# Opening of the attention stage: stack loads on two DMA queues, and half of the second group's row maxima inside the first group

## The chip, the cores and the metric

One Trainium2 core runs the whole program as one launch. The metric is device time in microseconds of the one core; lower is better. The kernel before was run three times for its time and once more under the profiler.

## The reference

Two transformer-like layers on `x[4, 512, 256]` (4 batches, 512 positions, width 256, 16 heads of 16). Layer 0 is softmax attention with a linear-attention memory term mixed in by a gate, plus a mixture of 8 experts (top 2). Layer 1 is decayed linear attention in chunks of 128, plus another mixture of 8 experts (top 2):

```
xn = layernorm(x)
q, k, v = rope(xn Wq), rope(xn Wk), xn Wv                   # layer 0
mem     = elu1(q) (elu1(k)^T v) / (elu1(q) sum elu1(k))
attn    = softmax(q k^T * 16**-0.5) v                       # per batch and head, 512 x 512 scores
x = x + (g * mem + (1 - g) * attn) Wo + moe0(xn)
xn = layernorm(x)
x = x + lightning_attention(xn) Wo1 + moe1(xn)              # layer 1
```

The change touches only the softmax attention of layer 0. Its softmax is computed as exp(score - row maximum), and the row maxima are computed first, by a pass of its own over the same scores.

## The kernel before

The program has three stages with a barrier of all engines between them: `layer0_front` (layer norm, projections, rotary, the first experts), `middle` (the softmax attention of layer 0, and for each batch what follows it up to the projections of layer 1), and `layer1_main`. The second stage, `middle`, is the one that changes, and of it only the opening.

**Work of the stage.** A batch has `GROUPS = 4` groups of `HG = 4` heads, and a group has `TILES = 4` tiles of 128 positions. Queries and keys are kept as stacks of three bfloat16 parts: `qst[g]` and `kst[g]`, 96 partitions (six pieces of 16) by 4 heads by 512 positions. One stack is loaded by six DMAs of 64 KB; the values `vst[g]` by one DMA of 256 KB. All 13 raise the same semaphore `stack_in[g]`, and `LOADED = 16 * 13` is what a reader waits for.

For each group n there are two passes on TensorE:

- `rows(n, g, t, b, heads)` (line 1491): for tile t, one matmul of 96 x 512 for each head into one of the two banks of `psM`; VectorE's `reduce(n, i, t)` (line 1305) takes the maximum of each row. A bank is free again when its maximum is taken. After four tiles (16 maxima) `split_max` (lines 1313 and 1315) makes two bfloat16 parts of them, TensorE's `turn_max` (line 1498) transposes these into `psN`, VectorE copies them to `nmT` (line 1466 or 1328), and SyncE's `send_max` stores `nmT` to memory (line 1087), waits, and loads it back as two further rows of `qst[g]` (line 1089, semaphore `max_in[g]`).
- `attend(b, g, ...)` on TensorE waits for `max_in[g]`. For each tile k it forms `scores` (line 1509, heads 0 and 1, then 2 and 3), ScalarE takes the exponential (line 1242), and `values(k - 1)` (line 1518) multiplies the tile before by the values.

The loop looks ahead by two groups: while group G is attended, the rows and maxima of group G + 2 are made, two heads behind each pair of scores. So the first two groups' maxima (groups 0 and 1) have to be made in front of the loop:

```
            for t in range(TILES):
                rows(0, 0, t, 0, range(HG))
            pe.wait_ge(identb_done, 1)
            for t in range(TILES):
                rows(1, 1, t, 0, range(HG))
                if t == 0:
                    turn_max(0, 0)
```

**Order on SyncE** (all loads are issued there): group 0's stacks and values, the identity matrix, group 1's stacks and values, seven small constants (`consts_in`, the last is `gates`), `iota8`, seven weights (`weights_in`), three tables (`dispatch.load`), group 2's stacks and values, `send_max` for group 0, group 3's stacks and values, and then the loop.

**Beside it.** ScalarE waits for the constants, forms `gates` (line 1285), the decay tables (lines 1287 to 1291) and, after `weights_in`, three rounded copies of the weights (line 1295). GpSimd sets parts of `kst` to one, issues eight indirect gathers (`fetch(0)`, line 1189), forms the low parts of the weights (line 1224, semaphore `w_lo`, three in all) and then masks the decay table (line 1227). VectorE, behind the maxima of both groups, takes 1 minus the gates (line 1469) and waits for `tables` and for all three of `w_lo` before it enters the loop.

Of the kernel before, what the change touches and what calls it, by code (L numbers as in the profile page):

```python
# [24 lines left out]
TILES = SEQ // P  # L25
D = 256
KT = D // P
HEADS = 16
HD = D // HEADS
HG = 4  # L30
GROUPS = HEADS // HG
# [18 lines left out]
Q_PARTS = (0, 0, 1, 0, 2, 1)  # L50
# [78 lines left out]
class Routing:  # L129
# [17 lines left out]
    def load(self, sp, io):  # L147
        sp.dma_start(self.iota8[:, :, :], io["iota8"].rearrange("p (t e) -> p t e", e=E)).then_inc(self.iota_in, 16)
# [795 lines left out]
def middle(nc, io, scratch, keep):  # L944
# [8 lines left out]
    with ExitStack() as ctx:  # L953
# [110 lines left out]
        def second(n):  # L1064
            return psM if alone(n) else psX

        block = ctx.enter_context(nc.Block())

        @block.sync
        def _(sp):  # L1070
            def load(b, g):
                for op, dst, order in ((0, qst, Q_PARTS), (1, kst, K_PARTS)):
                    for i, part in enumerate(order):
                        row = (g % 2) * HG * HD
                        src = scratch["parts"][b, part, KT * op + g // 2, row:row + HG * HD, :]
                        sp.dma_start(dst[g][i * HD:(i + 1) * HD, :, :],
                                     src.rearrange("(h d) t -> d h t", d=HD)).then_inc(stack_in[g], 16)
                sp.dma_start(vst[g][:, :, :], scratch["v"][b, :, g * HG * VW:(g + 1) * HG * VW]
                             .rearrange("(t p) n -> p t n", p=P)).then_inc(stack_in[g], 16)

            def send_max(n, g, i, before=None):

                sp.wait_ge(nmT_copied, n)
                if before is not None:
                    sp.wait_ge(max_in[(g - 1) % GROUPS], before)

                sp.dma_start(scratch["max"], nmT[i][:, :]).then_inc(max_out, 16)
                sp.wait_ge(max_out, 16 * n)
                sp.dma_start(qst[g][STACK:STACKM, :, :],
                             scratch["max"].rearrange("(a h) t -> a h t", a=2)).then_inc(max_in[g], 16)  # L1090

            load(0, 0)
            sp.dma_start(ident[:, :], io["ident"]).then_inc(ident_in, 16)
            load(0, 1)
            for dst, src in ((after[:, :], io["after"]), (rel[:, :], io["rel"]), (causal[:, :], io["causal"]),
                             (before[:, :], io["before"]), (ldrows[:, :], io["log_decay_rows"]),
                             (ldall[:, :], io["log_decay"].to_broadcast((P, HEADS))),
# [3 lines left out]
            for dst, src in ((rqk[:, :, 0:D], "Wq1"), (rqk[:, :, D:2 * D], "Wk1"), (rv, "Wv1"),  # L1101
                             (rr[:, :, 0:E], "router1"), (rr[:, :, E:RW], "Wg1"),
                             (wo[:, :, :], "Wo0")):
                sp.dma_start(dst, io[src].rearrange("(k p) n -> p k n", p=P)).then_inc(weights_in, 16)
            sp.dma_start(wg2[:, :], io["Wg2"]).then_inc(weights_in, 16)
            dispatch.load(sp, io)
            load(0, 2)
            send_max(1, 0, 0)
            load(0, 3)

            def attend(b, g, last, beside):
# [120 lines left out]
        def _(act):  # L1232
# [46 lines left out]
            def silu_v(n):  # L1279
                act.wait_ge(v_ps, n + 1)  # L1280
                nc.scalar.activation(v32[:, :, :, 0:HD], second(n)[:, :, :].rearrange("p a (t h d) -> p (a t) h d", t=2, d=HD),
                                     ACT.Silu).then_inc(v_done, 1)

            act.wait_ge(consts_in, CONSTS)
            nc.scalar.activation(gates[:, 1, :], gates[:, 1, :], ACT.Sigmoid).then_inc(g_done, 1)
            for k in range(KT):
# [13 lines left out]
        def _(dve):  # L1300
# [17 lines left out]
            def attend(b, g, last, beside):  # L1318
                G = GROUPS * b + g
                ahead = not (last and g >= GROUPS - 2)  # L1320
                for t in range(TILES):
                    if ahead:
                        reduce(G + 2, g % 2, t)
                    if t == 0 and not (last and g == GROUPS - 1):

                        dve.wait_ge(max_out, 16 * G)
                        dve.wait_ge(nmT_ready, G + 2)
                        nc.vector.tensor_copy(nmT[(g + 1) % 2][:, :], psN[0:2 * HG, :]).then_inc(nmT_copied, 1)
                    beside(t)
                    if t == TILES - 1 and ahead:  # L1330
                        split_max(G + 2, g % 2)
                dve.wait_ge(probs_used, TILES * (G + 1))
                if g == 0:
                    dve.wait_ge(heads_ps, TILES * b)
                nc.vector.tensor_copy(outT[:, g, :], psV[:, :]).then_inc(out_copied, 1)
# [123 lines left out]
            for t in range(TILES):  # L1459
                reduce(0, 0, t)  # L1460
            split_max(0, 0, reused=False)
            for t in range(TILES):
                reduce(1, 1, t)
                if t == 0:
                    dve.wait_ge(nmT_ready, 1)
                    nc.vector.tensor_copy(nmT[0][:, :], psN[0:2 * HG, :]).then_inc(nmT_copied, 1)
            split_max(1, 1, reused=False)
            dve.wait_ge(g_done, 1)
            nc.vector.tensor_scalar(gates[:, 0, :], gates[:, 1, :], -1.0, 1.0, ALU.mult, ALU.add).then_inc(omg_done, 1)
            dve.wait_ge(omg_done, 1)  # L1470
# [13 lines left out]
        def _(pe):  # L1484
# [17 lines left out]
            def attend(b, g, last, beside):  # L1502
                G = GROUPS * b + g
                pe.wait_ge(max_in[g], 16 * b + 16)

                def scores(k, heads):
                    for h in heads:
                        pe.wait_ge(scores_used[h % 2], 2 * (TILES * G + k) + h // 2)
                        nc.tensor.matmul(psE[h % 2][:, :], kst[g][0:STACKM, h, k * P:(k + 1) * P],  # L1509
                                         qst[g][0:STACKM, h, :], start=True, stop=True).then_inc(scores_ready, 1)  # L1510

                def values(k):
                    for used in scores_used:
                        pe.wait_ge(used, 2 * (TILES * G + k + 1))
                    if k == 0:
                        pe.wait_ge(out_copied, G)
                    for h in range(HG):
                        mm = nc.tensor.matmul(psV[VW * h:VW * (h + 1), :], vst[g][:, k, VW * h:VW * (h + 1)],  # L1518
                                              probs[k % PSLOTS][:, h, :], start=k == 0, stop=k == TILES - 1,
                                              tile_position=(0, VW * h), skip_group_check=True)  # L1520
                    mm.then_inc(probs_used, 1)

                for k in range(TILES):
                    ahead = not (last and g >= GROUPS - 2)
                    next_rows = G + 2, (g + 2) % GROUPS, k, b if g < 2 else b + 1
                    scores(k, (0, 1))
                    if k == 1 and not (last and g == GROUPS - 1):
                        turn_max(G + 1, (g + 1) % 2)
                    if ahead:
                        rows(*next_rows, (0, 1))  # L1530
                    if k:
                        values(k - 1)
                    scores(k, (2, 3))
                    beside(k)
                    if ahead:
                        rows(*next_rows, (2, 3))
                values(TILES - 1)


# [112 lines left out]
            for t in range(TILES):  # L1652
                rows(0, 0, t, 0, range(HG))
            pe.wait_ge(identb_done, 1)
            for t in range(TILES):
                rows(1, 1, t, 0, range(HG))
                if t == 0:
                    turn_max(0, 0)
            pe.wait_ge(ones, GROUPS)

            def ready():
# [551 lines left out]
```

## Time and profile before

| | |
|---|---|
| three runs, us | 1004.47, 997.73, 994.32 (median 997.73) |
| the profiled execution, us | 995.28, span 993.4 from the first to the last instruction |
| mean granted TensorE clock | 0.913 of 2.4 GHz |
| busy, share of the span | TensorE 84%, VectorE 58%, ScalarE 40%, GpSimd 31% |
| second stage | from 201.2 us of the span; first scores at 233.1 us |

The span runs on one time axis for all engines. A busy share is an average over three stages with different limits, so a stretch has to be read by itself. Transfers are seen in two ways: as the time for which an engine's queue (SPq is SyncE's, POOLq is GpSimd's) is occupied by issuing them, and as the time from issue to landing. PE is TensorE's matmuls, PEld its loading of weights, DVE VectorE, ACT ScalarE, POOL GpSimd.

### The profile page before, as it was taken

What the parts mean: (1) busy time and instruction counts of PE and PEld (TensorE: products, weight loads), DVE (VectorE), ACT (ScalarE), POOL (GpSimd) and SP (SyncE); (2) the same over time, 40 slices, a digit from 0 to 9 for tenths busy, and PEclk for the clock granted to TensorE, in tenths of its full rate; (3) what the DMA queues carried; (4) which work ended last, traced back from release to release, by engine and by line L of the source; (5) the groups of instructions that cost most, each with busy time, mean ns of one, the idle gap of its engine ahead of it and who ended that gap; (6) DMA issues with size and microseconds to landing.
All of it is one profiled execution on the core that took longest, in us unless ns stands there. A gap on an engine that the chain in (4) does not pass through costs nothing. (4 is left out here: it accounts for less than half of the span.)

```text
span 993.4 us, 14867 instructions
## 1 busy us (share of the span) xinstructions
PE 837.8 (84%) x4544; PEld 486.6 (49%) x4544; DVE 573.7 (58%) x1269; ACT 394.2 (40%) x676; POOL 311.4 (31%) x250
## 2 busy tenths in 40 slices
PE   4989999848998987997988748399799999999990
PEld 4765655501223443433434436256566666666660
DVE  7746877258779776777674435424343443444435
ACT  2336666414555565466446604022122222222220
POOL 3033567363001330151015113214243344344230
PEclk9999999956999997999798966599899999999995
DMA  8514655463222323533403301799773344344007
GB/s 273 136 59 146 198 184 183 151 187 92 86 67 61 117 85 100 170 106 107 145 27 107 127 21 61 213 288 307 209 171 99 92 125 115 90 116 124 23 16 259
DMA packets 158353, 130.26 MB, mean 131 GB/s; under 512 B 64128, under 2 KB 139920, under 8 KB 158288
## 3 DMA queue, kind: packets, MB, share of 16 engines
q1 hardware_dynamic: 151136, 109.89, 37.6%
q0 software_dynamic: 7152, 19.54, 6.7%
q8 instruction: 37, 0.61, 0.3%
q14 instruction: 28, 0.23, 0.1%
HBM read 83.37 MB, written 46.01 MB: 130 GB/s over the span
## 5 line engine op out<-in xcount | busy, mean ns | idle before, releaser
L1305 DVE TENSOR_REDUCE b_negmax<-b_psM 128x1 f32<-128x512 f32 x256 | 163.0, 683 | 61.0 <-PE b_psM L1491 58.2
L1242 ACT ACTIVATE b_probs<-b_psE 128x512 f32<-128x512 f32 x256 | 138.8, 594 | 125.9 <-PE b_psE L1509 125.1
L1491 PE MATMUL b_psM<-b_kst,b_qst 96*128 96x512 bf16 x256 | 98.5, 427 | 42.1 <-DVE b_negmax L1305 26.0
L1509 PE MATMUL b_psE<-b_qst,b_kst 98*128 98x512 bf16 x256 | 87.9, 405 | 14.1 <-ACT b_probs L1242 9.6
L2007 PE MATMUL d_psG<-d_w,d_xT 128*128 x156 | 76.9, 616 | 2.5 <-issue 1.4
L1860 POOL DMA_INDIRECT scratch_ys<-d_y,put x39 | 39.7, 1018 | 122.4 <-ACT d_y L1891 120.8
L2032 PE MATMUL d_psY<-d_w,d_hidden 128*128 x312 | 76.8, 390 | 0.8 <-ACT d_hidden L1885 0.8
L2015 PE MATMUL d_psU<-d_w,d_xT 128*128 x156 | 75.0, 603 | 0.0
L1491 PEld LDWEIGHTS b_psM<-b_kst,b_qst 96*128 96x128 bf16 x256 | 24.5, 99 | 101.4 <-DVE b_negmax L1305 76.7
L1518 PE MATMUL b_psV<-b_probs,b_vst 128*32 128x512 f32 x512 | 71.9, 634 | 2.5 <-ACT b_probs L1242 2.5
L1509 PEld LDWEIGHTS b_psE<-b_qst,b_kst 98*128 98x128 bf16 x256 | 20.4, 98 | 101.0 <-issue 51.8
L1865 POOL TENSOR_TENSOR d_rs<-d_ss,d_neghalf 128x16 f32<-128x16 f32 x16 | 46.9, 2933 | 67.5 <-DVE d_ss L1949 67.5
L1891 ACT ACTIVATE d_y<-d_psY 128x256 f32<-128x256 f32 x39 | 15.0, 384 | 129.9 <-PE d_psY L2032 129.9
L1879 ACT ACTIVATE d_hidden<-d_psG 128x512 f32<-128x512 f32 x39 | 23.3, 597 | 107.1 <-PE d_psG L2007 107.1
L2032 PEld LDWEIGHTS d_psY<-d_w,d_hidden 128*128 128x128 f32 x312 | 58.6, 194 | 14.4 <-issue 7.8
L527 POOL DMA_INDIRECT a_xg<-scratch_xn,a_take x39 | 42.0, 1076 | 73.6 <-PE a_psXH L886 48.4
L1914 DVE TENSOR_TENSOR d_hidden<-d_hidden,d_psU 128x512 f32<-128x512 f32 x39 | 26.8, 688 | 65.9 <-PE d_psU L2015 65.9
L1919 DVE TENSOR_TENSOR d_probs<-d_ps,decay 128x512 f32<-128x512 f32 x64 | 43.9, 688 | 35.9 <-PE d_ps L2047 34.6
L1170 POOL TENSOR_TENSOR b_combined<-b_both 128x256 f32<-128x256 f32 x16 | 11.6, 725 | 154.2 <-DVE b_both L1349 154.2
L896 PE MATMUL a_psV<-a_w,a_xgT 128*128 x156 | 54.1, 470 | 4.4 <-issue 3.8
L915 PE MATMUL a_psV<-a_w,a_hT 128*128 (+1 forms) x156 | 49.6, 417 | 3.7 <-ACT a_hT L610 3.7
L1851 POOL DMA_INDIRECT d_xg<-scratch_xn,take x39 | 38.3, 983 | 34.2 <-POOLq L76 15.6
(353 smaller groups left out, 1591.0 us busy)
## 6 DMA issues: line engine op xcount, KB each, us to landing
scratch_parts<-a_parts SPq DMA_DIRECT2D x12, 512.0 KB, 4.2
b_qst<-scratch_parts SPq DMA_DIRECT2D x96, 64.0 KB, 2.1
b_kst<-scratch_parts SPq DMA_DIRECT2D x96, 64.0 KB, 2.1
scratch_parts<-b_part SPq DMA_DIRECT2D x24, 256.0 KB, 3.1
d_qst<-scratch_parts SPq DMA_DIRECT2D x96, 64.0 KB
d_kst<-scratch_parts SPq DMA_DIRECT2D x96, 64.0 KB
scratch_ys<-a_y SPq DMA_DIRECT2D x39, 128.0 KB, 1.8
scratch_v<-a_xn SPq DMA_DIRECT2D x4, 1024.0 KB, 6.9
```

The source lines that it names most:

```text
L896: mm = nc.tensor.matmul(psM[:, b % 2, 0:2 * F0], xgT[b % 2][:, k, :], w[:, bass.ds(owner[b], 1), at:at + 2 * F0].rearrange("p a n -> p (a ...
L915: mm = nc.tensor.matmul(psY[:, 0:D], hTall[0:rows, b % 2, k, :], w[0:rows, bass.ds(owner[b], 1), at:at + D].rearrange("p a n -> p (a n)"), ...
L1242: nc.scalar.activation(probs[k % PSLOTS][:, h, :], psE[h % 2][:, :], ACT.Exp, scale=float(HD) ** -0.5).then_inc(scores_used[h % 2], 1)
L1305: nc.vector.tensor_reduce(negmax[i][:, t, h:h + 1], psM[:, h % 2, :], AX_X, ALU.max, negate=True).then_inc(rows_used[h % 2], 1)
L1491: nc.tensor.matmul(psM[:, h % 2, :], qst[g][0:STACK, h, t * P:(t + 1) * P], kst[g][0:STACK, h, :], start=True, stop=True).then_inc(rows_re ...
L1509: nc.tensor.matmul(psE[h % 2][:, :], kst[g][0:STACKM, h, k * P:(k + 1) * P], qst[g][0:STACKM, h, :], start=True, stop=True).then_inc(score ...
L1518: mm = nc.tensor.matmul(psV[VW * h:VW * (h + 1), :], vst[g][:, k, VW * h:VW * (h + 1)], probs[k % PSLOTS][:, h, :], start=k == 0, stop=k = ...
L1865: nc.gpsimd.tensor_tensor(rs[:, :], ss[:, :], neghalf[:, :], ALU.pow).then_inc(rs_done, 1)
L1919: nc.vector.tensor_tensor(probs[g][:, :], (ps1 if g % 2 else ps0)[:, :], decay[:, HG * g:HG * g + HG, :].rearrange("p h c -> p (h c)"), AL ...
L2007: mm = nc.tensor.matmul(psG[:, :], xT[b % 2][:, k, :], weights(b, GATE + k * H1, H1), start=k == 0, stop=k == KT - 1)
L2015: mm = nc.tensor.matmul(psU[:, :], xT[b % 2][:, k, :], weights(b, UP + k * H1, H1), start=k == 0, stop=k == KT - 1)
L2032: mm = nc.tensor.matmul(psY[:, 0:D], hT[b % 2][:, k, :], weights(b, DOWN + k * D, D), start=k == 0, stop=k == HT1 - 1)
```

## The change

1. A helper `load_stack` loads one stack on an engine's queue. The key stacks of groups 0, 1 and 2 are issued from ScalarE's queue, in front of everything else that ScalarE does in the stage; the query stacks stay on SyncE.
2. SyncE's order in the opening becomes: query stack 0, identity, query stack 1, values 0, values 1, query stack 2, values 2, constants, `iota8`, weights, `send_max` for group 0, the three tables, group 3.
3. Of group 1's maxima, tiles 0 and 1 stay in front of the loop. Tiles 2 and 3 and the group's `split_max` move into the first tile of group 0 (`opening(b, g)`). Group 2's tiles 0 and 1 are both made in the second tile of group 0; from the third tile on the order is that of before. In the two altered tiles TensorE issues the four extra row matmuls (`catch_up`) at the end of the tile. The copy of group 1's `nmT` on VectorE moves from behind one set of four maxima to behind the first two altered tiles' sixteen.

```
+        def load_stack(eng, b, g, op, dst, order):
+            for i, part in enumerate(order):
+                row = (g % 2) * HG * HD
+                src = scratch["parts"][b, part, KT * op + g // 2, row:row + HG * HD, :]
+                eng.dma_start(dst[g][i * HD:(i + 1) * HD, :, :],
+                              src.rearrange("(h d) t -> d h t", d=HD)).then_inc(stack_in[g], 16)
+        def opening(b, g):
+            return isinstance(b, int) and b == 0 and g == 0
...
-            load(0, 0)
+            load_stack(sp, 0, 0, 0, qst, Q_PARTS)
             sp.dma_start(ident[:, :], io["ident"]).then_inc(ident_in, 16)
-            load(0, 1)
+            load_stack(sp, 0, 1, 0, qst, Q_PARTS)
+            load_values(0, 0)
+            load_values(0, 1)
+            load_stack(sp, 0, 2, 0, qst, Q_PARTS)
+            load_values(0, 2)
...
+            send_max(1, 0, 0)
             dispatch.load(sp, io)
-            load(0, 2)
-            send_max(1, 0, 0)
             load(0, 3)
...
+            for g in range(3):
+                load_stack(act, 0, g, 1, kst, K_PARTS)
             act.wait_ge(consts_in, CONSTS)
...
                 for t in range(TILES):
-                    if ahead:
+                    if opening(b, g):
+                        if t == 0:
+                            reduce(1, 1, 2)
+                            reduce(1, 1, 3)
+                            split_max(1, 1, reused=False)
+                        elif t == 1:
+                            reduce(2, 0, 0)
+                            reduce(2, 0, 1)
+                        else:
+                            reduce(2, 0, t)
+                    elif ahead:
                         reduce(G + 2, g % 2, t)
-                    if t == 0 and not (last and g == GROUPS - 1):
+                    if t == (1 if opening(b, g) else 0) and not (last and g == GROUPS - 1):
...
-            for t in range(TILES):
-                reduce(1, 1, t)
-                if t == 0:
-                    dve.wait_ge(nmT_ready, 1)
-                    nc.vector.tensor_copy(nmT[0][:, :], psN[0:2 * HG, :]).then_inc(nmT_copied, 1)
-            split_max(1, 1, reused=False)
+            reduce(1, 1, 0)
+            dve.wait_ge(nmT_ready, 1)
+            nc.vector.tensor_copy(nmT[0][:, :], psN[0:2 * HG, :]).then_inc(nmT_copied, 1)
+            reduce(1, 1, 1)
...
+                    catch_up = ()
+                    if opening(b, g) and k == 0:
+                        next_rows, catch_up = (1, 1, 2, 0), ((1, 1, 3, 0),)
+                    elif opening(b, g) and k == 1:
+                        next_rows, catch_up = (2, 2, 0, 0), ((2, 2, 1, 0),)
...
                     if ahead:
                         rows(*next_rows, (2, 3))
+                    for late in catch_up:
+                        rows(*late, range(HG))
...
-            for t in range(TILES):
-                rows(1, 1, t, 0, range(HG))
-                if t == 0:
-                    turn_max(0, 0)
+            rows(1, 1, 0, 0, range(HG))
+            turn_max(0, 0)
+            rows(1, 1, 1, 0, range(HG))
```

## Rows read from the trace of the kernel before

**Rows 1.** Windows: each engine's busy us (instructions), granted clock, DMA share, GB/s.
```profile
204.00:207.00 3.00, 0.00 (x0) 0.00 (x0) 0.00 (x0) 0.00 (x0) 3.00 (x3) 0.50 0.47 132
...
219.00:222.00 3.00, 2.54 (x5) 0.42 (x5) 2.75 (x6) 1.61 (x3) 0.95 (x1) 0.50 0.93 276
...
242.00:244.00 2.00, 2.00 (x12) 0.31 (x4) 0.39 (x2) 0.44 (x1) 0.00 (x0) 0.77 0.02 4
```

**Rows 2.** Timeline of TensorE's row matmuls and what followed, opening and group 0.
```profile
209.94 1.04 PE L1491 MATMUL b_psM<-b_kst,b_qst 96*128 96x512 bf16 x2 [12.84 <-DMA b_vst<-scratch_v]
...
231.41 1.21 PE L1491 MATMUL b_psM<-b_kst,b_qst 96*128 96x512 bf16 x2 [0.18 <-DVE b_negmax L1305]
233.11 1.01 PE L1509 MATMUL b_psE<-b_qst,b_kst 98*128 98x512 bf16 x2 [0.49 <-issue]
233.92 1.06 PE L1491 MATMUL b_psM<-b_kst,b_qst 96*128 96x512 bf16 x2
237.94 1.21 PE L1491 MATMUL b_psM<-b_kst,b_qst 96*128 96x512 bf16 x2 [2.11 <-DVE b_negmax L1305]
...
241.42 1.79 PE L1518 MATMUL b_psV<-b_probs,b_vst 128*32 128x512 f32 x8
...
244.22 0.88 PE L1509 MATMUL b_psE<-b_qst,b_kst 98*128 98x512 bf16 x2
```

**Rows 3.** Timeline of SyncE's queue in the opening: what it issued, and for how long.
```profile
201.22 2.95 SPq L1076 DMA_DIRECT2D b_qst<-scratch_parts  x6
...
207.03 0.43 SPq L1078 DMA_DIRECT2D b_vst<-scratch_v  x1
207.50 0.50 SPq L1093 DMA_DIRECT2D b_ident<-in_ident_dram  x1
...
217.07 0.43 SPq L1099 DMA_DIRECT2D b_gates<-in_gate_attn_dram  x1
...
229.09 0.45 SPq L1087 DMA_DIRECT2D scratch_max<-b_nmT  x1
231.48 0.24 SPq L1089 DMA_DIRECT2D b_qst<-scratch_max  x1
...
241.07 0.28 SPq L1087 DMA_DIRECT2D scratch_max<-b_nmT  x1
242.35 0.25 SPq L1089 DMA_DIRECT2D b_qst<-scratch_max  x1
```

**Rows 4.** DMA issues of 190 to 260 us: size of one, median us to landing.
```profile
b_qst<-scratch_parts SPq DMA_DIRECT2D x30, 64.0 KB, 2.2
...
b_vst<-scratch_v SPq DMA_DIRECT2D x5, 256.0 KB, 2.9
...
b_outT<-in_Wk_dram SPq DMA_DIRECT2D x1, 256.0 KB, 4.0
```

**Rows 5.** Timeline of VectorE in the opening and in group 0.
```profile
210.59 11.04 DVE L1305 TENSOR_REDUCE b_negmax<-b_psM 128x1 f32<-128x512 f32 x16 [0.26 <-PE b_psM L1491]
...
224.64 0.40 DVE L1466 COPY b_nmT<-b_psN 8x512 bf16<-8x512 bf16 x1
...
233.45 3.42 DVE L1313 CAST b_nmparts<-b_negmax 128x16 bf16<-128x16 f32 x1
...
241.10 1.29 DVE L1305 TENSOR_REDUCE b_negmax<-b_psM 128x1 f32<-128x512 f32 x2
244.00 2.64 DVE L1305 TENSOR_REDUCE b_negmax<-b_psM 128x1 f32<-128x512 f32 x4 [1.61 <-PE b_psM L1491]
```

**Rows 6.** Timeline of ScalarE and GpSimd in the opening.
```profile
220.36 0.22 ACT L1285 ACTIVATE b_gates<-b_gates 128x16 f32<-128x16 f32 x1 [17.86 <-DMA b_gates<-in_gate_attn_dram]
...
232.33 4.51 POOL L1227 TENSOR_TENSOR decay<-decay,b_causal 128x2048 f32<-128x2048 f32 x1
```

**Rows 7.** Line 1313, all its instructions: ns min/median/max of one.
```profile
L1313 DVE CAST b_nmparts<-b_negmax x16: 164/168/3415, 221.7 to 523.8; 128x16 bf16<-128x16 f32 x16
```

**Rows 8.** Timeline of SyncE's queue early in the third stage.
```profile
651.78 4.99 SPq L1794 DMA_DIRECT2D d_qst<-scratch_parts  x6
```

More of the change, by code:

```diff
@@ L1070, in _, with load_values, load @@
         def _(sp):
[L1071 to L1077, printed above, removed]
+            def load_values(b, g):
                 sp.dma_start(vst[g][:, :, :], scratch["v"][b, :, g * HG * VW:(g + 1) * HG * VW]
                              .rearrange("(t p) n -> p t n", p=P)).then_inc(stack_in[g], 16)
+            def load(b, g):
+                load_stack(sp, b, g, 0, qst, Q_PARTS)
+                load_stack(sp, b, g, 1, kst, K_PARTS)
+                load_values(b, g)
             def send_max(n, g, i, before=None):
```

## The prediction

> **What bounds the kernel now.** The busy shares of the page are a mean of three stages, so I started from the order of work. The change touches only the opening of the second stage, and the stages are divided by barriers, so what it is worth is how much earlier or later TensorE comes to the point from which the two kernels do the same work. That point is the third tile of group 0, whose scores start at 244.22 us [rows 2]; from there each tile is one set of four maxima, two sets of scores and one of values, as before.
>
> I then read the opening engine by engine. TensorE waits 12.84 us for its first row matmul, at 209.94, and what ends the wait is the load of the values, not a stack [rows 2]: all 13 loads of a group raise one semaphore. From there VectorE sets the pace: 16 maxima take 11.04 us, 0.69 each, without a gap [rows 5], and TensorE idles 0.18 us in front of each pair of row matmuls to let it keep up [rows 2]. Group 1's maxima go on like this until 233.4. The first scores start at 233.11, right behind the last rows (231.41 and 1.21) [rows 2]. Then VectorE stands still: the cast of group 1's maxima lasts 3.42 us [rows 5] where the median of the 16 such casts is 0.168 [rows 7]; it ends at 236.87, and GpSimd's masking of the decay table ends at 236.84 [rows 6]. TensorE waits 2.11 us for it in the first tile of group 0 [rows 2].
>
> So the 34 us between the first maximum (210.59) and the third tile are VectorE's: 40 maxima by 0.69 are 27.6 us, the rest is that cast and shorter waits.
>
> **The first loads.** Six stack DMAs occupy SyncE for 2.95 us [rows 3], 0.47 each from start to start, and land 2.2 us after issue [rows 4]. With the key stacks on ScalarE's queue, both stacks of group 0 should land near 206.5. But the first row matmul waits for the values too. They are now behind six query DMAs, the identity and six more query DMAs: 201.22 + 12 x 0.47 + 0.54 = 207.4 to 207.55, against 207.03 [rows 3]. So the second queue brings nothing for the first rows; it is 0.5 us the other way. To this comes crowding. One queue gives a DMA share of 0.47 and 132 GB/s (204 to 207); two would ask for twice that, 0.94, and 0.93 with 276 GB/s is about the most of this opening [rows 1]. A 256 KB load there took 4.0 us to land, against 2.9 for the values [rows 4]. The values therefore land 0.5 to 1.6 us later than before; I take +1.0, as the crowding has only begun by then. First maximum at 211.6.
>
> The Trainium skill has a rule that speaks against the change: "DMA: Bandwidth & Descriptors", section "Issuing engines are not separate DMA queues", says that issuing from several engines saves only sequencer time, which is usually small beside the transfer. Here the trace disagrees with the second half: six issues take 2.95 us and one lands in 2.2, so issue time is the larger; by the rule alone the stacks would come no earlier, and the sum would be the same, because the values decide.
>
> **Maxima in front of the loop.** 16 maxima, 11.04: to 222.6. Group 0's `nmT` copy ended at 225.04 before [rows 5], so now at 226.0; tile 1 of group 1 ends four maxima later, at 228.8. This takes 8 maxima (5.5 us) from in front of the first scores.
>
> **The maxima's trip.** Before, `nmT` was ready at 225.04, but SyncE was still issuing group 2's loads and sent it at 229.09, and waited 2.39 us for the store [rows 3]. Now SyncE stands ready and little else is in flight, so the store should take what the next trip took, 1.28 us (241.07 to 242.35) [rows 3], and the way back at most the 1.63 from 231.48 to the scores at 233.11 [rows 2, 3]: 226.0 + 1.3 + 1.6 = 228.9. TensorE is free at about 229.3. First scores at 229.3, 3.8 us earlier than before; with a 2.39 us store, at 230.1.
>
> **Where that gain goes.** Three things stand in the way.
>
> First, VectorE waits for all three `w_lo` before it enters the loop. Before, it came there last (at 237) and the wait cost nothing; now it comes at 228.9. The chain behind `w_lo` is ScalarE's, from the gates' landing (220.36) to the masking that follows GpSimd's third low part (232.33) [rows 6], 12.0 us. In the new order SyncE issues 18 query DMAs, the identity, three values and six constants ahead of the gates: 18 x 0.47 + 0.54 + 3 x 0.47 + 6 x 0.475 = 13.3, so at 214.5 against 217.07 [rows 3], 2.6 earlier. `w_lo` is complete at 229.8 if the gates land as fast as before, and up to 1.7 us later if they queue. I take 230.6. The 18 issues on ScalarE itself are hidden: ScalarE waits until 220.36 [rows 6], and 18 by 0.47 are over at 209.7. Without that cover they would cost 8.5 us.
>
> Second, the remaining rows of group 1 now stand behind the first scores in TensorE's queue, and these wait for the trip. One pair of scores to the next instruction is 0.81 us, and the first row matmul needs another 0.6 [rows 2]: 229.3 + 1.4 = 230.7. Rows for heads 2 and 3 stand behind two pairs of scores, which puts in about 0.5 us of idle VectorE. (Before, rows needed no trip.)
>
> Third, all the work that was taken away comes back inside: tile 0 holds 8 maxima and not 4, tile 1 as well. 230.7 + 0.5 + 8 x 0.69 = 236.7, and 0.35 for the two instructions of `split_max`: 237.1. The long cast goes away: the decay mask starts at `w_lo` and ends 4.5 us later, near 235.1, before the cast starts. If it did not go, up to 3.4 us would be back.
>
> The Trainium skill explains that cast: "SBUF — State Buffer", section "Who interferes with whom", has the SBUF ports that VectorE shares with GpSimd as an exclusive lock, which a plain cast can need and a max reduction from PSUM does not. The trace agrees, 3.42 against 0.168 us; by it the order decides, and since eight maxima stand between `w_lo` and the cast, the sum is as above.
>
> Then tile 1. Rows follow the transposes by 0.5 us and the first maximum comes 0.65 later (209.94 to 210.59 [rows 2, 5]): 238.3. `values(0)` comes about 1.5 us behind the transposes and takes 1.79 at the low clock [rows 2]: until 240.4. Scores and the next row matmul take 0.4 to 0.8 more, and the following maximum starts at 241.2 to 241.6. Before, the same maximum (tile 1, head 2) started at 244.00, and TensorE's third tile began 0.22 us later [rows 2, 5]. Now six maxima of group 2's two tiles are left: the last row matmul can go when the fourth of them is taken, 241.4 + 4 x 0.66 = 244.0, and the third tile's scores follow at about 244.6 to 244.8.
>
> **Sum.** Third tile at about 244.7 against 244.22: **+0.5 us**. The 3.8 us gained at the first scores and the 3.4 us of the cast go to the wait for `w_lo`, to the later start, and to eight maxima that now stand inside group 0. Group 1's `nmT` was sent at 241.07 [rows 3]; now the copy stands behind tile 1's maxima, at about 245.5. Its trip (2.9 us) is over at 248.5, and group 1 can't start before two more tiles of some 3.5 us, 251.7, so it is hidden, with 3 us to spare. On the profiled execution's 995.28 us this is 995.8. The median of the three runs is 997.73 and they lie between 994.32 and 1004.47; a run that is shown with the change will lie within that scatter, so I name 997.
>
> **Bounds of the shift.** Low end: values +0.5, `w_lo` at 229.8, no idle between maxima, clock up a little sooner: the restart at 229.9 instead of 230.7, and 0.5 less: -0.8. High end: trip slow (230.1) and `w_lo` at 231.5, tile 1 wholly at the low clock: +0.8 and +0.8, so +2.1.
>
> **Rivals.**
>
> A, the change pays. The clock is 0.50 until about 242.9 (0.77 over 242 to 244) [rows 1], some 5 us after TensorE's last long gap (until 237.94) [rows 2]. With scores from 229.3 and no 2.11 us gap, it may be granted by 236. Then `values(0)` takes about half, 0.9 us less, and each pair of scores or rows some 0.4 less: with the low end, some -2.5 us: 992.8, or 994.5 as named from the median. For it: TensorE is fuller. Against it: with VectorE at 0.69 us a maximum, TensorE was busy to 2.54 of 3 us and stayed at 0.50 [rows 1], and eight more matmuls keep that pace. 20%.
>
> B, slower: the two queues crowd each other. Early in the third stage six stack DMAs took SyncE 4.99 us [rows 8], 0.83 each against 0.47. If both queues issue at that pace from the first stack on, the values leave 12 x 0.36 = 4.3 us later, and the gates 18 x 0.36 = 6.5 us later. `w_lo` is then complete at 236.3 and all behind it moves by 5.6: +6, 1001.5. It decides from about 0.55 us an issue, where `w_lo` (18 x 0.08) passes 231.5. For it: the share asked for is 0.94, and an issue can take 0.83. Against it: the gates' issue at 217.07, with much in flight, took 0.43 [rows 3]. 13%.
>
> C, slower: the clock comes late. If TensorE is still at half clock through tiles 2 and 3, with four pairs at 0.81 (233.11 to 233.92) and values at 1.79 [rows 2], a tile takes 5.0 us. At full clock half of that and 1.0 us for issue, an estimate, make 3.5. So it is +3.0 for two tiles and +0.8 for tile 1, so +4.3 with the sum: 999.6, or 1001.3 from the median. For it: the catch-up rows of tile 1 again run at VectorE's pace. 12%.
>
> D, the change does not do what it says: the first rows do not come earlier at all. It is part of the forecast (the values decide).
>
> **Chances.** The forecast's mechanism with its bounds 55%, A 20%, B 13%, C 12%. None of them alone reaches 1% (10 us), which is about what a measurement can tell from no change here, since the three runs before spread by 10 us. What could reach it is a scatter of that kind, or B and C together, +10. So within 1% 92%, faster 3%, slower 5%. Range: from A with a fast run, 992, to B and C's middle with the upper half of the scatter, 1003.
>
> **What would show each step.** First row matmul at 210.4 to 211.5, still ended by the values. First scores at 229 to 230. Cast of group 1's maxima at 0.17 us. VectorE idle between 228.8 and 230.7, with GpSimd's line 1224 ending just before it goes on. Third tile's scores at 244 to 246. DMA share over 0.85 from 204 on. The prediction is wrong if the stacks' issues take 0.6 us or more, if the wait for `w_lo` is not there, or if the clock rises more than 3 us away from 241.

## The result and the profile after

The changed kernel takes 1006.9 us (median of 18 runs, 996.3 to 1016.1) against 997.4 (18 runs). The ratio is 1.0068, 95% interval 1.0035 to 1.0101: some 6.8 us slower. It is smaller than that of the medians (9.5 us), because ratios here leave out the executions that ran over 1.5% longer than their kernel's fastest. The prediction was 997, range 992 to 1003.

The profiled execution's span is 1002.3 us against 993.4. The first stage, which is the same program in both, ended 3.9 us later in this one: SyncE's first issue of the second stage is at 205.16 and not 201.22. That is scatter (the kernels below have it anywhere from 200.0 to 206.5), so from here on all times with a plus sign are counted from that first issue. The second scores of group 0's third tile (in the tables below "3rd tile"), the first instructions at which both kernels do the same at full clock, come at +45.4 before (246.66) and at +52.8 after (258.00): **7.4 us later**. Of the 8.9 us of the two spans, 3.9 are scatter and 7.4 the opening; the rest of the program gave 2.4 back.

The queues' timeline of the changed kernel, beside [rows 3]:

```profile
205.16 2.68 SPq L1071 DMA_DIRECT2D b_qst<-scratch_parts  x6
...
211.65 0.98 SPq L1082 DMA_DIRECT2D b_vst<-scratch_v  x2
...
216.04 2.47 SPq L1112 DMA_DIRECT2D b_after<-in_after_dram  x1
...
221.94 1.19 SPq L1112 DMA_DIRECT2D b_gates<-in_gate_attn_dram  x1
...
235.28 0.34 SPq L1096 DMA_DIRECT2D scratch_max<-b_nmT  x1
236.57 0.23 SPq L1098 DMA_DIRECT2D b_qst<-scratch_max  x1
```
```profile
205.16 8.99 ACTq L1071 DMA_DIRECT2D b_kst<-scratch_parts  x18
```

Both queues issue the pieces of the stacks at the old pace, 0.45 to 0.50 us each, so the values are issued at +6.5 against +5.8. But see when they land (issues of the opening, last column us to landing), against 2.2 and 2.9 in [rows 4]:

```profile
b_kst<-scratch_parts ACTq DMA_DIRECT2D x18, 64.0 KB, 4.3
b_qst<-scratch_parts SPq DMA_DIRECT2D x18, 64.0 KB, 3.8
b_vst<-scratch_v SPq DMA_DIRECT2D x3, 256.0 KB, 8.5
b_gates<-in_gate_attn_dram SPq DMA_DIRECT2D x1, 8.0 KB, 7.3
```

The windows of +3 to +12 and +12 to +20, of the kernel before and then of the changed one, tell why; the last two columns are the DMA share and GB/s:

```profile
204.22:213.22 9.00, 2.73 (x5) 0.45 (x5) 2.75 (x5) 0.00 (x0) 7.62 (x11) 0.50 0.64 178
213.22:221.22 8.00, 6.79 (x13) 1.20 (x12) 7.39 (x13) 0.85 (x2) 5.52 (x6) 0.50 0.87 235
```
```profile
208.16:217.16 9.00, 0.00 (x0) 0.00 (x0) 0.26 (x1) 1.28 (x1) 7.62 (x11) 0.50 1.16 149
217.16:225.16 8.00, 4.28 (x8) 0.76 (x8) 4.05 (x7) 0.00 (x0) 5.53 (x6) 0.50 1.12 248
```

With two queues the DMA share is 1.16 and the bytes are fewer, 149 GB/s, than with one queue at a share of 0.64 (178). So the share does not tell how many bytes move: a second queue of requests brought fewer, and everything behind them waited, the values first of all. TensorE's timeline:

```profile
220.15 1.04 PE L1513 MATMUL b_psM<-b_kst,b_qst 96*128 96x512 bf16 x2 [19.82 <-DMA b_vst<-scratch_v]
...
238.15 1.01 PE L1531 MATMUL b_psE<-b_qst,b_kst 98*128 98x512 bf16 x2 [0.90 <-issue]
...
242.19 1.21 PE L1513 MATMUL b_psM<-b_kst,b_qst 96*128 96x512 bf16 x2 [1.32 <-DVE b_negmax L1319]
...
248.94 1.94 PE L1540 MATMUL b_psV<-b_probs,b_vst 128*32 128x512 f32 x8
250.81 0.61 PE L1531 MATMUL b_psE<-b_qst,b_kst 98*128 98x512 bf16 x2
...
254.61 1.06 PE L1531 MATMUL b_psE<-b_qst,b_kst 98*128 98x512 bf16 x2
...
256.46 1.61 PE L1540 MATMUL b_psV<-b_probs,b_vst 128*32 128x512 f32 x8
```

First row matmul at +15.0 (before +8.7 [rows 2]), first scores at +33.0 (before +31.9), third tile at +49.45 (before +43.0). So the 8 maxima taken from in front of the first scores hide nearly all of the 6.3 us that the loads cost there, and then it comes out again inside the group. VectorE, ScalarE and GpSimd, in that order (compare [rows 5, 6]):

```profile
220.80 11.04 DVE L1319 TENSOR_REDUCE b_negmax<-b_psM 128x1 f32<-128x512 f32 x16 [6.05 <-PE b_psM L1513]
...
237.90 1.91 DVE L1491 TENSOR_SCALAR b_gates<-b_gates 128x16 f32<-128x16 f32 x1
241.44 5.47 DVE L1319 TENSOR_REDUCE b_negmax<-b_psM 128x1 f32<-128x512 f32 x8 [1.64 <-POOL b_wr L1236]
247.02 0.17 DVE L1327 CAST b_nmparts<-b_negmax 128x16 bf16<-128x16 f32 x1
```
```profile
229.23 0.22 ACT L1299 ACTIVATE b_gates<-b_gates 128x16 f32<-128x16 f32 x1 [13.76 <-DMA b_gates<-in_gate_attn_dram]
```
```profile
241.20 4.50 POOL L1239 TENSOR_TENSOR decay<-decay,b_causal 128x2048 f32<-128x2048 f32 x1
```

The gates landed at +24.1, before at +19.1; the chain behind them ends with the low weight parts at +36.1, 12.0 us behind the gates as before, and right then VectorE goes on, at +36.3. The 3.42 us cast [rows 5] is 0.17.

### The profile page after: what moved, and what is told of

It reads as the page before. It is cut to its first block and busy times, and to the rows that moved or that the text cites. A ratio compares the mean times of both kernels' runs of the same rounds, so it can differ in the third digit from the quotient of the medians.

```text
span 1002.3 us, 14867 instructions
## 1 busy us (share of the span) xinstructions
PE 840.9 (84%) x4544; PEld 486.0 (48%) x4544; DVE 574.1 (57%) x1269; ACT 393.9 (39%) x676; POOL 311.0 (31%) x250
## 5 line engine op out<-in xcount | busy, mean ns | idle before, releaser
L1540 PE MATMUL b_psV<-b_probs,b_vst 128*32 128x512 f32 x512 | 74.7, 657 | 3.0 <-ACT b_probs L1254 3.0
```

## The experiments

Three landmarks are taken from each kernel's profile: first row matmul, first scores, and second scores of the third tile of group 0, all from SyncE's first issue in the second stage (that issue's own time in the last column), and the ratio to the kernel before on the same chip.

```
kernel                            rows    scores  3rd tile  ratio (95% interval)      issue at
before                            +8.7    +31.9   +45.4                                201.22
changed                           +15.0   +33.0   +52.8     1.0068 (1.0035, 1.0101)    205.16
e1_loads_only                     +14.6   +37.1   +50.9     1.0033 (1.0006, 1.0060)    201.97
e2_maxima_only                    +8.5    +31.7   +51.2     1.0044 (1.0011, 1.0076)    201.71
e3_keys_apart                     +11.2   +29.2   +49.0     1.0058 (1.0022, 1.0094)    200.04
e4_values_first                   +8.9    +27.9   +52.2     1.0083 (1.0050, 1.0115)    205.91
e5_maxima_early_trip              +8.5    +26.5   +48.4     1.0031 (1.0000, 1.0063)    203.43
e6_constants_first                +8.5    +31.0   +44.1     1.0002 (0.9971, 1.0032)    204.75
e7_group0_two_queues              +7.0    +29.5   +42.3     0.9968 (0.9938, 0.9998)    201.37
e8_group0_two_queues_moved        +6.8    +24.9   +44.5     1.0006 (0.9976, 1.0035)    204.00
e9_keys_32_off                    +15.1   +33.0   +52.8     one run, no ratio          202.87
e10_mask_later_before             +8.7    +31.7   +41.1     0.9946 (0.9905, 0.9987)    202.47
e11_two_queues_mask_later         +6.9    +29.4   +41.1     0.9954 (0.9909, 0.9999)    206.52
```

0.1% is 1 us. The ratios follow the third tile within their intervals, which are 5 to 9 us wide; the landmarks are the finer measure of the opening.

**The two halves alone.** e1 keeps the loads and puts the maxima back:

```diff
         def opening(b, g):
-            return isinstance(b, int) and b == 0 and g == 0
+            return False
...
-            reduce(1, 1, 0)
-            dve.wait_ge(nmT_ready, 1)
-            nc.vector.tensor_copy(nmT[0][:, :], psN[0:2 * HG, :]).then_inc(nmT_copied, 1)
-            reduce(1, 1, 1)
+            for t in range(TILES):
+                reduce(1, 1, t)
+                if t == 0:
+                    dve.wait_ge(nmT_ready, 1)
+                    nc.vector.tensor_copy(nmT[0][:, :], psN[0:2 * HG, :]).then_inc(nmT_copied, 1)
+            split_max(1, 1, reused=False)
```
(and the same on TensorE). Expected:

> Only the loads of the change: both queues and the new order on SyncE, with the maxima of the kernel before. Times are counted from SyncE's first issue of the stage. Theory 1 (the two queues crowd each other, and the maxima's move costs nothing of its own): the first row matmul comes at 15.0 us as in the changed kernel and not at 8.7 as before, the DMA share is over 1.1 at about 145 GB/s from 3 to 12 us, and the whole is 6 to 7 us slower than before. Rival 2 (the maxima's move carries the loss): first row matmul still late, but 3 us or more of the 6.8 us come back, because VectorE no longer waits for the low weight parts with eight maxima still to do: the whole is at most 3.5 us slower than before.

Rows at +14.6, 154 GB/s at a share of 1.15: as theory 1 has it. The opening is 5.5 us longer than before; the whole, 3.3 us (interval 0.6 to 6.0), is less than the 6 to 7 expected, and within rival 2's bound, so the time alone speaks for rival 2 and decides little. The landmark divides the loss: 5.5 of the 7.4 us come with the loads alone, and with these loads the moved maxima cost a further 52.8 - 50.9 = 1.9 us. Theory 1's second half, that the move costs nothing of its own, is wrong.

e2 is the other half, the maxima moved and every load as before:

```diff
-            load_stack(sp, 0, 0, 0, qst, Q_PARTS)
+            load(0, 0)
             sp.dma_start(ident[:, :], io["ident"]).then_inc(ident_in, 16)
-            load_stack(sp, 0, 1, 0, qst, Q_PARTS)
-            load_values(0, 0)
-            load_values(0, 1)
-            load_stack(sp, 0, 2, 0, qst, Q_PARTS)
-            load_values(0, 2)
+            load(0, 1)
...
-            send_max(1, 0, 0)
             dispatch.load(sp, io)
+            load(0, 2)
+            send_max(1, 0, 0)
...
-            for g in range(3):
-                load_stack(act, 0, g, 1, kst, K_PARTS)
```

> Only the maxima's move; all loads and the trip of group 0's maxima as in the kernel before. Theory 1: first row matmul at 8.7 us. The trip is sent at 27.9 us as before, so the first scores stay at 31.9, VectorE is idle from 26.9 to about 33.3 (rows now stand behind the scores), and the third tile of group 0 comes at about 47 us and not at 43.0: 3 to 4 us slower than before, which would mean that the move is worth nothing without an earlier trip. Rival 2 (the move is harmless or pays by itself, since the long cast goes): third tile at 43 us or earlier, no change of time or a gain of up to 3 us.

Slower by 4.4 us, and the third tile's first scores at +47.5, both as theory 1 had it. VectorE's timeline in e2 shows the price of putting rows behind scores that wait for the maxima's trip:

```profile
227.90 0.17 DVE L1486 TENSOR_SCALAR b_gates<-b_gates 128x16 f32<-128x16 f32 x1
234.97 1.29 DVE L1314 TENSOR_REDUCE b_negmax<-b_psM 128x1 f32<-128x512 f32 x2 [6.90 <-PE b_psM L1508]
```

It stands for 6.90 us with half of group 1 still to do. So either half loses alone (both intervals lie above 1), and the changed kernel is not a good idea spoilt by the other half.

**Why two queues move fewer bytes.** e3 changes only the order of ScalarE's six pieces. A query stack's piece i and a key stack's piece i both go to partitions 16 i to 16 i + 15 of their tiles, and the two queues issue them at the same time.

```diff
-            for i, part in enumerate(order):
+            for i in ((4, 5, 1, 0, 3, 2) if apart else range(6)):
+                part = order[i]
```
(with `apart=True` in ScalarE's call).

> The changed kernel with one edit: ScalarE issues the six pieces of a key stack in the order 4, 5, 1, 0, 3, 2 and not 0 to 5, so that at no time a query piece and a key piece go to the same 16 partitions. Bytes, sizes, queues and counts are the same. Theory 1a (the pieces in flight at one time land on the same partitions, and that is what halves the rate): 3 to 12 us after the stage's start the rate rises from 145 GB/s to over 190, the values land in 3 to 5 us and not 8.5, first row matmul at 10 to 12 us. Theory 1b (two queues with twice the requests fill the DMA engines, whatever the partitions): rate, landing and first row matmul (15.0 us) stay within 0.5 us of the changed kernel's.

e9 is the same edit with the order 2, 3, 0, 1, 4, 5, so that the first four pairs lie 32 partitions apart and the last two on the same ones.

> The changed kernel with ScalarE's key pieces in the order 2, 3, 0, 1, 4, 5, so that for four of the six pairs the query and the key piece go to partitions that differ by 32, and for the last two to the same ones. If what crowds is the very same partitions at one time, most of the rate comes back, as with the order 4, 5, 1, 0, 3, 2: over 190 GB/s from 3 to 12 us and the first row matmul at 11 to 12.5 us. If what crowds is a path into the memory that partitions 32 apart have in common, the rate stays near 150 GB/s and the first row matmul at 14 to 15.5 us. The Trainium skill, page SBUF — State Buffer, section Door 1: The DMA port swizzle, states the second: partitions 32 apart are behind the same port.

The windows of +3 to +12, of e3 and then of e9:

```profile
203.04:212.04 9.00, 0.83 (x2) 0.13 (x2) 0.88 (x2) 1.28 (x1) 7.62 (x11) 0.50 1.12 227
```
```profile
205.87:214.87 9.00, 0.00 (x0) 0.00 (x0) 0.23 (x1) 1.28 (x1) 7.62 (x11) 0.50 1.16 148
```

Same bytes, same queues, same counts: 227 GB/s against 148, and the values landed in 5.0 us in e3 against 8.5 in the changed kernel. Theory 1a holds. e9 gives the changed kernel's rate to 1 GB/s and its landmarks to 0.1 us. Four of its six pairs no longer share partitions, so the very same partitions are hardly what matters; a path that partitions 32 apart have in common fits both runs. Both edits also change the order in which the parts are read from memory, and e9, which gains nothing, speaks against that as the cause. The pairs are exact for group 0 only: behind the identity and the values SyncE runs up to three pieces behind ScalarE.

By the Trainium skill, page "SBUF — State Buffer", section "Door 1: The DMA port swizzle", 16 partitions reach 4 of 16 ports and were measured at 104 GB/s, and partition p + 32 lies behind p's port; e3 and e9 agree with the map, and the changed kernel's 149 GB/s, in which other transfers have a part, are nearer to that figure than to the rate of the pieces apart.

Even apart the crowd costs 2.5 us at the first rows (+11.2 against +8.7). The constants profit as well: in e3 each is issued in 0.43 to 0.51 us again, the gates at +13.5, and the low weight parts are complete at +31.9 and not +36.1. VectorE of e3 goes on right behind them:

```profile
232.18 5.47 DVE L1320 TENSOR_REDUCE b_negmax<-b_psM 128x1 f32<-128x512 f32 x8 [1.63 <-POOL b_wr L1237]
```

**Where the wait sits in the queue.** e4 issues group 0's values right behind its query stack:

```diff
             load_stack(sp, 0, 0, 0, qst, Q_PARTS)
+            load_values(0, 0)
             sp.dma_start(ident[:, :], io["ident"]).then_inc(ident_in, 16)
             load_stack(sp, 0, 1, 0, qst, Q_PARTS)
-            load_values(0, 0)
```

> The changed kernel with the values of group 0 issued right behind its query stack, ahead of the identity and of group 1's queries. Theory 1 (the values wait in their queue behind the crowded stacks): with six stacks in front and not twelve, the values land 4 to 5 us after an issue at 2.8 us, so the first row matmul comes at 7 to 8.5 us, before the 8.7 of the kernel before. The constants stay behind the crowd, so the low weight parts come at 36 us as in the changed kernel, VectorE waits for them, and the third tile of group 0 gains little: 48 to 49.5 us. Rival 3 (the first rows' delay sets the whole opening): all of the 7 us come back, third tile at 42 to 43 us.

Rows at +8.9, later than the 7 to 8.5 expected, and of the 6.1 us gained there the third tile keeps 0.6: theory 1's 48 to 49.5 for its first scores (+48.8) holds, and rival 3 falls. VectorE of e4:

```profile
241.58 5.47 DVE L1319 TENSOR_REDUCE b_negmax<-b_psM 128x1 f32<-128x512 f32 x8 [8.62 <-POOL b_wr L1236]
```

It now waits 8.62 us for the low weight parts. The opening is bound by the chain from the constants' landing to these parts, no longer by the first loads. The changed kernel, e3, e4, e5, e8 and e9 all show it: VectorE goes on right behind the low weight parts (+36.3, +32.1, +35.7, +31.6, +27.6 and +36.3, in that order), and the third tile's first scores follow 13.1 to 13.6 us later.

**Does the move pay with an early trip?** e5 is e2 with group 0's trip ahead of group 2's loads, and the three tables behind them:

```diff
-            dispatch.load(sp, io)
-            load(0, 2)
             send_max(1, 0, 0)
+            load(0, 2)
+            dispatch.load(sp, io)
```

> The maxima's move with the loads of the kernel before on SyncE alone, but the trip of group 0's maxima sent ahead of group 2's loads. Theory 4 (the move pays nothing even with an early trip, because VectorE then stands at the low weight parts): first row matmul at 8.7 us, first scores at 27 to 28 us, VectorE idle from 26.5 to about 31 (the weight parts are complete at 30.7 to 31.1), second scores of the third tile at 47 to 48.5 us, against 45.4 before and 51.2 with the move alone. Rival 5 (an early trip is all that the move lacked): 44.5 us or earlier.

First scores at +26.5 (27 to 28 expected), 5.4 us earlier than before, and the third tile still 3.0 us later: theory 4. VectorE of e5 waits 5.12 us, now for the weight parts:

```profile
234.99 5.47 DVE L1314 TENSOR_REDUCE b_negmax<-b_psM 128x1 f32<-128x512 f32 x8 [5.12 <-POOL b_wr L1233]
```

**The constants, and a second queue for one stack.** e6 is the kernel before with another order on SyncE, e7 adds a second queue for group 0's keys alone, in e3's order, e8 adds the moved maxima and the early trip to e7. SyncE's order in short, not code:

```diff
+            load_stack(sp, 0, 0, 0, qst, Q_PARTS)       # e7: keys 0 on ScalarE, order 4, 5, 1, 0, 3, 2
+            load_values(0, 0)                           # (e6: load(0, 0))
             ident
+            constants
             load(0, 1)
-            constants
             iota8, weights
+            load(0, 2)
+            send_max(1, 0, 0)
             tables
-            load(0, 2)
-            send_max(1, 0, 0)
```

> The kernel before (its maxima, one queue), with the seven constants issued ahead of group 1's loads, and group 0's trip sent between group 2's loads and the three tables. Theory 4: the gates land near 12.5 us, the low weight parts are complete at about 28.5 to 29 and the mask of the decay table ends near 33, so the long cast of group 1's maxima lasts 1 to 1.5 us and not 3.4, and the third tile's second scores come at 43 to 44 us, 1.5 to 2.5 us earlier than before. Rival 5 (the loss of the change has nothing to do with when the constants come): no change, 45.4.

> As the run with constants first, and in addition group 0's key stack alone on ScalarE's queue, its pieces in the order 4, 5, 1, 0, 3, 2, and group 0's values right behind its query stack. The maxima are in the order of the kernel before. Theory 4 with theory 1a: first row matmul at 6.3 to 7.3 us against 8.7, low weight parts complete at 26 to 27, mask over near 31, cast of group 1's maxima under 1.5 us, second scores of the third tile at 41 to 42 us: 3.5 to 4.5 us faster than before, if the rest of the program keeps its time. Theory 1b (any second queue crowds): first row matmul not before 8.7.

> The run before this one with the maxima moved as in the change, and the trip sent ahead of group 2's loads. Theory 4 (the move itself never gains here): first scores near 25 us, but eight maxima more behind them and the catch-up rows keep VectorE and TensorE in step: second scores of the third tile at 43 to 44 us, 1.5 to 2.5 us later than without the move. Rival 5 (with early loads and constants the move pays): 40.5 us or earlier.

e6's cast took 2.28 us and not the 1 to 1.5 expected, the third tile came 1.3 us earlier (1.5 to 2.5 expected), and no change of the time can be told: a gain too small for its interval. e7 is faster than the kernel before by 3.2 us (interval 0.2 to 6.2), which is what its third tile says, 3.1; both are a little under what was expected, as its cast took 2.41 us and not under 1.5. A second queue helps the opening when it carries one stack and what the first rows wait for stands in front: rows at +7.0 against +8.5 in e6, third tile at +42.3 against +44.1. By the time of the whole, e6 and e7 can't be told apart. e8 differs from e7 in the moved maxima and the trip: its first scores are 4.6 us earlier and its third tile 2.2 us later (+44.5, 43 to 44 expected). So in none of the three pairs (e1 and changed, before and e2, e7 and e8) does the move gain anything, and it costs 1.9 to 5.8 us.

The granted clock shows a part of that cost. One-microsecond windows of the changed kernel at +45, +49, +51 and +53, then of e8 before its fall, in it and behind it, and of e7 (the granted clock is the third column from the end):

```profile
250.16:251.16 1.00, 1.00 (x6) 0.21 (x3) 0.00 (x0) 0.00 (x0) 0.00 (x0) 0.69 0.00 0
254.16:255.16 1.00, 0.95 (x3) 0.40 (x4) 0.90 (x2) 0.00 (x0) 0.00 (x0) 0.52 0.00 0
256.16:257.16 1.00, 1.00 (x5) 0.20 (x8) 1.00 (x2) 0.27 (x1) 0.00 (x0) 0.50 0.03 8
258.16:259.16 1.00, 0.96 (x5) 0.28 (x3) 0.30 (x1) 0.73 (x2) 0.00 (x0) 1.00 0.00 0
```
```profile
244.00:245.00 1.00, 0.58 (x3) 0.18 (x3) 1.00 (x3) 0.00 (x0) 0.00 (x0) 1.00 0.26 75
246.00:247.00 1.00, 1.00 (x6) 0.31 (x9) 1.00 (x4) 0.71 (x2) 0.00 (x0) 0.50 0.00 0
249.00:250.00 1.00, 0.96 (x5) 0.25 (x3) 0.41 (x1) 0.84 (x2) 0.00 (x0) 1.00 0.00 0
```
```profile
239.37:240.37 1.00, 1.00 (x9) 0.11 (x2) 0.43 (x1) 0.00 (x0) 0.00 (x0) 0.90 0.00 0
245.37:246.37 1.00, 0.97 (x7) 0.27 (x10) 0.94 (x2) 0.97 (x2) 0.00 (x0) 1.00 0.00 0
```

In the kernels with moved maxima the clock rises to 2.4 GHz in tile 1, falls back to 1.2 for about 3 us and rises again; in e2 it rises only at +51. In before, e1, e6, e7, e10 and e11 it rises once and stays. What differs just before the fall are the catch-up rows of tile 1, single matmuls of 0.39 us with 0.21 idle, waiting for VectorE (TensorE busy 0.58 of the microsecond at 244.00 in e8). The tile after that runs at half clock: `values(1)` takes 1.61 us, 1.07 in the kernel before. That the catch-up rows cause the fall was not tried by itself, and e11 has two such single matmuls in its tile 1 and keeps the clock.

**The cast that waits for the mask.** e10 is the kernel before with one line more, e11 is e7 with the same line:

```diff
             pool.wait_ge(tables, TABLES)
+            pool.wait_ge(omg_done, 1)
```

> The kernel before with one wait more: GpSimd's mask of the decay table waits until VectorE has taken 1 minus the gates, which is behind group 1's split. Theory 4: the cast of group 1's maxima takes 0.17 us and not 3.42, the mask runs beside the maxima of tile 0, which it doesn't hinder, and the second scores of the third tile come at 42 to 43 us and not 45.4: 2.5 to 3.3 us faster. Rival 6 (the cast only fills time in which VectorE would wait for something else): 45 us, no change.

> Group 0's keys alone on ScalarE's queue, constants first, the maxima of the kernel before (the faster version found so far, second scores of the third tile at 42.3 us), and the mask of the decay table behind the split as in the run beside it. Theory 4: the cast, 2.41 us there, takes 0.17 us, second scores of the third tile at 39.8 to 40.5 us, 5 to 5.6 us earlier than in the kernel before, and 5 to 5.5 us faster on the whole. Rival 6: 42.3 us, no gain over the run without it.

The cast in e10 (VectorE's timeline), and the mask (GpSimd's):

```profile
234.65 0.18 DVE L1314 CAST b_nmparts<-b_negmax 128x16 bf16<-128x16 f32 x1
```
```profile
235.29 4.53 POOL L1228 TENSOR_TENSOR decay<-decay,b_causal 128x2048 f32<-128x2048 f32 x1 [2.34 <-DVE b_gates L1470]
```

3.42 us became 0.18 at the same place; the third tile comes 4.3 us earlier, more than the 2.5 to 3.3 expected; beside the missing cast, TensorE has no gap there and the clock rises at +35 and not at +41.5. On the whole e10 is 5.4 us faster than the kernel before (interval 1.3 to 9.5), the lowest ratio of this study, with its one line; the intervals of e7 and e11 overlap its own. e11 missed its 39.8 to 40.5: it starts 2.3 us earlier, but its tile 1 runs at half clock (`values(0)` 1.94 us against 1.06 in e10) and it arrives at the same +41.1. Its ratio is the same within the intervals, so no gain of the second queue on top is shown. Its trace is of one execution of 1014.6 us, and its executions spread from 998.6 to 1018.3, so the clock seen there may not stand for the others.

## Why the prediction was wrong

- **What bounds the opening.** Right: the values end the first wait (19.82 us idle, released by them), VectorE sets the pace, and the long cast goes. Its 40 maxima in front of the third tile are two too many, as 38 had been taken by then (26.2 us and not 27.6); no term of the sum uses them.
- **The crowding of the two queues: the step that failed.** It let the share of two queues be the sum of two, 0.94, still under the most of the opening, and so sized two terms too small. The first is the values' landing, taken as at most 4.0 us from a 256 KB load of weights at a share of 0.93: it took 8.5 us, and the rows came 6.3 us later, not 1.0. The runs show in its place a share of 1.16 with 149 GB/s, and 227 GB/s once the pieces go to other paths. That both stacks go to the same partitions piece by piece could be read in the code: `dst[g][i * HD:(i + 1) * HD]` for both.
- **`w_lo`, the second of these terms and the one that sets the time.** The wait was foreseen, but the parts were to be complete at +29.4 and came at +36.1. The gates were issued at +16.8 and not +13.3, as the constants' issues, 0.43 to 0.51 us each before, took up to 2.47, and they landed in 7.3 us and not 3.3. In e3, with the pieces on other paths, the gates left at +13.5, about as predicted, and the parts came at +31.9. e4 shows which term counts: with the rows 6.1 us earlier the third tile gains 0.6.
- **The trip and the work inside the group.** Right in kind and size: the store took 1.29 us (1.28 predicted), and from VectorE's restart to the third tile it was 13.2 us, 14.0 predicted. With the restart at +36.3 in place of +29.5, the predicted +0.5 becomes 0.5 + 6.8 - 0.8 = 6.5, which is what the third tile's first scores show (+49.45 against +43.0).
- **The clock** is the last microsecond: neither rival A (an early rise) nor C (late) but up, down and up again.
- **Rival B** had nearly the right sum, +6, and half of the mechanism: the stacks' issues, on which it rested, did not get slower (0.50 and 0.46 us a piece), but those of the constants did, and the landings, which it left as they were, took the rest. A chance of 13% on "the two queues crowd each other" was too small.
- **The sign.** The forecast was no change within 1%, which is where the ratio lies. But the shift that the bounds allowed, 2.1 us, was a third of the true one. With 6.8 us on 997.4 the kernel is at 1004.2, just outside the range; the median, 1006.9, lies a further 2.7 us out.

What stays open: the changed kernel's third tile is 7.4 us late and e3's 3.6, while their ratios differ by 1 us only; the intervals are too wide to say whether the rest of the program adds anything. No run has the new order on SyncE without the second queue. No run has both the early trip and low weight parts that are complete before VectorE needs them, so it is not shown that the move can't gain there. What makes the clock fall again is open too.

## What to carry to other kernels

Before a second DMA queue is given half of a set of loads, look at which partitions the pieces go to at the same moment: here two queues in step on the same 16 partitions, or mostly on ones 32 apart, moved fewer bytes than one queue did, and the values behind them took three times as long to land. A load that is counted in the same semaphore as the stacks belongs in front of the next group's, though e4 shows that this alone gave the whole nothing. Work moved from in front of a wait to behind it gained nothing here, where another chain (constants, decay tables, low weight parts) ended later, so find what is late next. And a tiny VectorE cast that takes 20 times its median beside a GpSimd operation was worth at least as much here, with one line, as the reordering around it (third tile 4.3 us earlier in e10, 3.1 in e7).

## What the runs showed of the hardware

- Two queues writing 64 KB pieces to 16 partitions each, over +3 to +12: 149 GB/s at a DMA share of 1.16 with the pieces in step on the same partitions, 148 with four of six pairs 32 partitions apart, 227 at 1.12 in e3's order.
- A VectorE cast of 128 x 16 took 3.42, 2.22 (e1), 2.28 (e6) and 2.41 us (e7) where the mask ran beside it, each time ending within 0.05 us of the mask's end, and 0.17 to 0.21 elsewhere in these openings. The mask itself did not slow the maxima beside it (5.47 us for 8 in the changed kernel, 0.69 us each in the kernel before).
- The 1 minus gates operation, 0.17 us before, took 1.91 us in the changed kernel beside GpSimd's line 1236, and 0.17 in e2, where GpSimd was idle.
